# Earlier loads, two fences and moved buffers in an eight-core attention and feed-forward layer

## The reference

```python
D = 1024; H = 16; HIDDEN = 3072
# attention; its input is a normalised x
xn = layernorm(xin) * ln_g + ln_b
q = xn @ Wq.T + bq; k = xn @ Wk.T + bk; v = xn @ Wv.T + bv
q = softmax(q per head, over the head's 64 columns)
k = softmax(k, over the tokens)
attn = einsum('bnhd,bnhl->bhdl', k, v)      # one 64x64 matrix per head
y = einsum('bnhd,bhdl->bnhl', q, attn)
attn_out = xin + y
# layer
x = x + attn_out(xin = norm(x))
h = silu(norm(x) @ wg.T) * (norm(x) @ wu.T) # wg, wu, wd are int32, times 1/127
x = x + h @ wd.T
```

## Time and profile before

| | us |
|---|---|
| median of 2 runs | 4600.26 (4599.89 to 4600.62) |
| profiled execution, its own time | 4595.73 |
| span of that execution, slowest core (core 4) | 4594.2 |
| spans of the other cores | 4571.0 to 4594.0 |
| TensorE busy on core 4 | 3643.5 (79% of the span) |
| VectorE, ScalarE busy | 1269.6, 636.6 |

### The profile page before, as it was taken

How to read it: one execution, slowest core, us unless ns; L and a number is a source line. 1 busy time by engine, 2 the same in 40 slices (tenths; PEclk the granted TensorE clock), 3 DMA queues, 4 the chain that set the end, 5 groups by cost and what they waited for, 6 DMA issues and landing times.

```text
span 4594.2 us, 60873 instructions; the slowest of 8 cores (4571.0 to 4594.2 us)
## 1 busy us (share of the span) xinstructions
PE 3643.5 (79%) x22512; PEld 2464.3 (54%) x22800; DVE 1269.6 (28%) x3078; ACT 636.6 (14%) x1092; POOL 168.9 (4%) x295
## 2 busy tenths in 40 slices
PE   0369788866537888785254699999999999999998
PEld 0234334345533343345253477777777777777776
DVE  0232321234543213214254122222222222222222
ACT  0221221211112212211011000000000000000000
POOL 0000000000000000000000000000000000000000
PEclk9989899985558998896555799999999999999999
DMA  9721111143432112124843300000000000000000
GB/s 117 135 65 60 69 69 53 60 128 109 124 106 69 65 55 72 58 84 125 170 123 107 74 29 29 29 29 29 6 24 29 28 29 29 29 29 29 29 10 10
DMA packets 229040, 289.25 MB, mean 63 GB/s; under 512 B 83653, under 2 KB 182085, under 8 KB 226122
## 3 DMA queue, kind: packets, MB, share of 16 engines
q1 hardware_dynamic: 136218, 134.32, 10.6%
q0 software_dynamic: 33904, 136.33, 10.4%
q10 hardware_dynamic: 58624, 14.69, 2.0%
HBM read 167.86 MB, written 136.31 MB: 66 GB/s over the span
## 4 chain that ended last, share of the span: by engine, by line
PE 73%; DVE 11%; issue 4%; another core or an unknown queue 4%; ACT 3%; ACTq 2%; DMA 1%; DVEq 1%; SPq 1%; POOL 0%; POOLq 0%
PE pb L1051 29%; PE pb L604 14%; PE pb L1020 14%; PE pb L545 9%; DVE h_st L887 3%; PE pb L747 2%; ACTq L94 2%; PE pb L800 1%; DVE n_t L511 1%; DVE ek_r L739 1%; ACT h1n_t L907 1%; DVE xnT_lo L519 1%; DVE hnT_lo_st L818 1%; PE pb L731 1%
## 5 line engine op out<-in xcount | busy, mean ns | idle before, releaser
L1051 PE MATMUL pb<-hnT_hi_b,wgT 128*128 128x256 bf16 x3072 | 838.2, 273 | 48.2 <-DMA h_b<-s_h 48.2
L1051 PE MATMUL pb<-hnT_lo_b,wgT 128*128 128x256 bf16 x3072 | 838.2, 273 | 0.0
L1051 PE MATMUL pb<-hnT_hi_b,wuT 128*128 128x256 bf16 x3072 | 838.0, 273 | 0.0
L1051 PE MATMUL pb<-hnT_lo_b,wuT 128*128 128x256 bf16 x3072 | 838.0, 273 | 0.0
L1064 DVE SCALAR_TENSOR_TENSOR g_t<-pb,g_t 128x256 f32<-128x256 f32 x384 | 163.1, 425 | 1484.2 <-ACT g_t L1060 1423.5
L1060 ACT ACTIVATE g_t<-pb 128x256 f32<-128x256 f32 x384 | 147.2, 383 | 1859.4 <-PE pb L1051 1859.3
L1051 PEld LDWEIGHTS pb<-hnT_hi_b,wgT 128*128 128x128 bf16 x3072 | 300.9, 98 | 122.8 <-issue 48.8
L1051 PEld LDWEIGHTS pb<-hnT_lo_b,wgT 128*128 128x128 bf16 x3072 | 300.8, 98 | 74.3 <-issue 0.3
L1051 PEld LDWEIGHTS pb<-hnT_hi_b,wuT 128*128 128x128 bf16 x3072 | 300.9, 98 | 35.1
L1051 PEld LDWEIGHTS pb<-hnT_lo_b,wuT 128*128 128x128 bf16 x3072 | 300.9, 98 | 35.1
L545 PE MATMUL pb<-wvT_hi,xnT_hi 128*128 128x512 bf16 x486 | 168.8, 428 | 189.1 <-DVE v_stg L572 179.1
(11 more groups left out here) (150 smaller groups left out, 4448.1 us busy)
## 6 DMA issues: line engine op xcount, KB each, us to landing
x_r<-x SPq DMA_DIRECT2D x32, 512.0 KB, 4.0
s_r<-r_r POOLq DMA_DIRECT2D x32, 512.0 KB, 4.8
s_v<-v_stg POOLq DMA_DIRECT2D x32, 512.0 KB, 2.9
s_qT<-qT_stg POOLq DMA_DIRECT2D x64, 256.0 KB, 3.3
s_kT<-kT_stg POOLq DMA_DIRECT2D x64, 256.0 KB, 2.7
kTe<-s_kT SPq DMA_DIRECT2D x16, 1024.0 KB, 4.9
v_p<-s_v SPq DMA_DIRECT2D x16, 1024.0 KB, 6.0
qT_c<-s_qT SPq DMA_DIRECT2D x32, 512.0 KB, 6.8
```

The costliest lines, as they stand in the source:

```text
L1051: hc=hc, bsl=bsl, st=st, sp=sp: e.matmul(pb[bnk][:, 0:256], wtt[:, d, hc * 128:(hc + 1) * 128], xt.ap()[:, bsl, d, :], start=st, stop=sp),
```

## The change

- Two loads of x (the first two chunks of the first sequence) are put at the head of SyncE's queue, ahead of the identity, and `S1` uses them instead of its own.
- `pw_f` gets four slots instead of two; `ptmp` keeps two.
- Buffers of phase 3 move up so that they no longer overlap those of phase 2; wdT becomes one buffer of 24 columns, and the feed-forward's other buffers change places with it.
- The eight early wdT loads on ScalarE's queue are dropped; all 24 go to SyncE's queue behind the last fence.
- `prefetch_ffn_blocks`, called behind `emit_early_ffn_loads`, puts the hi and lo loads of blocks 0 and 1 on SyncE's queue at the end of phase 2 of the second sequence; the feed-forward uses them.
- The fence after phase 2 of the first sequence is dropped.

```diff
@@ buffers @@
-    qT_c = A("qT_c", [128, 2, 8, 128], F32, offset=P1 + 28 * KB)
-    r_c = A("r_c", [128, 2, D], F32, offset=P1 + 36 * KB)
-    h1_st = A("h1_st", [128, 2, D], F32, offset=P1 + 44 * KB)
-    h1n_t = A("h1n_t", [128, 2, D], F32, offset=P1)
+    qT_c = A("qT_c", [128, 2, 8, 128], F32, offset=P1 + 40 * KB)
+    r_c = A("r_c", [128, 2, D], F32, offset=P1 + 48 * KB)
+    h1_st = A("h1_st", [128, 2, D], F32, offset=P1 + 56 * KB)
+    h1n_t = A("h1n_t", [128, 2, D], F32, offset=P1 + 64 * KB)
...
-    pw_f = A("pw_f", [128, 2, D], F32, offset=P1 + 28 * KB)
+    pw_f = A("pw_f", [128, 4, D], F32, offset=P1 + 28 * KB)
...
-    wdT_a = A("wdT_a", [128, 8, D], BF16, offset=176 * KB)
-    wdT_b = A("wdT_b", [128, 16, D], BF16, offset=112 * KB)
-    hnT_hi_b = A("hnT_hi_b", [128, 2, 8, 256], BF16, offset=144 * KB)
-    hnT_lo_b = A("hnT_lo_b", [128, 2, 8, 256], BF16, offset=152 * KB)
+    hnT_hi_b = A("hnT_hi_b", [128, 2, 8, 256], BF16, offset=112 * KB)
+    hnT_lo_b = A("hnT_lo_b", [128, 2, 8, 256], BF16, offset=120 * KB)
+    wdT_t = A("wdT_t", [128, 24, D], BF16, offset=128 * KB)
...
@@ prologue @@
+    pre_x0 = {}
+    for c0 in range(2):
+        pre_x0[c0] = P.dma("sync", x0_r[:, c0, :], x_in[c0 * 128:(c0 + 1) * 128, :])
     m_ident = P.dma("sync", ident[:], ident_in[:, :])
...
-    pw_free = [[m_gcol], [m_bcolf]]
+    pw_free = [[m_gcol], [m_bcolf], [], []]
...
-            sl = (wi * 8 + rb) % 2
+            sl = (wi * 8 + rb) % 4
...
+            psl2 = sl % 2
...
@@ phase 1, S1 @@
-            mx = P.dma("sync", x0, x_in[tok0:tok0 + 128, :],
-                       waits=x0_res[sl].free)
+            if s == 0 and c < 2:
+                mx = pre_x0[c]
+            else:
+                mx = P.dma("sync", x0, x_in[tok0:tok0 + 128, :],
+                           waits=x0_res[sl].free)
...
@@ emit_early_ffn_loads @@
-        for hc in range(8):
-            mw[("d", hc)] = P.dma(
-                "scalar", wdT_a[:, hc, :], s_wd[0:D, hc * 128:(hc + 1) * 128],
-                waits=[m_cast["d"]] + deps, transpose=True)
...
+    def prefetch_ffn_blocks():
+        (ek_res2, kTe_res2, ekq_res2, vp_res2, _, _) = ph2_state[1]
+        ph2done = (vp_res2[0].free + vp_res2[1].free
+                   + kTe_res2[0].free + kTe_res2[1].free)
+        for b in range(2):
+            t0b = b * 256
+            mhi = P.dma("sync", hnT_hi_b[:, b % 2, :, :],
+                        s_hnT_hi[:, :, t0b:t0b + 256].transpose([1, 0, 2]),
+                        waits=m_hnT_store[b] + ph2done)
+            mlo = P.dma("sync", hnT_lo_b[:, b % 2, :, :],
+                        s_hnT_lo[:, :, t0b:t0b + 256].transpose([1, 0, 2]),
+                        waits=m_hnT_store[b] + ph2done)
+            ffn_pre[b] = [mhi, mlo]
@@ stages @@
             emit_early_ffn_loads()
+            prefetch_ffn_blocks()
             P.fence(pre)
+        elif nm.startswith("p2"):
+            pass
         else:
             P.fence()
...
@@ feed-forward @@
-    m_wd = {hc: mw[("d", hc)] for hc in range(8)}
-    for hc in range(8, 24):
+    m_wd = {}
+    for hc in range(24):
         m_wd[hc] = P.dma(
-            "sync", wdT_b[:, hc - 8, :], s_wd[0:D, hc * 128:(hc + 1) * 128],
+            "sync", wdT_t[:, hc, :], s_wd[0:D, hc * 128:(hc + 1) * 128],
             waits=[m_cast["d"]], transpose=True)
...
+        if b in ffn_pre:
+            mhi, mlo = ffn_pre[b]
+        else:
...
```

More of the change, by code:

```diff
@@ L246, in build @@
     wuT = A("wuT", [128, 8, HID], BF16, offset=64 * KB)
-    wdT_a = A("wdT_a", [128, 8, D], BF16, offset=176 * KB)
-    wdT_b = A("wdT_b", [128, 16, D], BF16, offset=112 * KB)
-    hnT_hi_b = A("hnT_hi_b", [128, 2, 8, 256], BF16, offset=144 * KB)
-    hnT_lo_b = A("hnT_lo_b", [128, 2, 8, 256], BF16, offset=152 * KB)
[L251 to L254, removed]
+    hnT_hi_b = A("hnT_hi_b", [128, 2, 8, 256], BF16, offset=112 * KB)
+    hnT_lo_b = A("hnT_lo_b", [128, 2, 8, 256], BF16, offset=120 * KB)
+    wdT_t = A("wdT_t", [128, 24, D], BF16, offset=128 * KB)
+    g1_t = A("g1_t", [128, 2, 256], F32, offset=176 * KB)
+    hmT_hi = A("hmT_hi", [128, 4, 256], BF16, offset=178 * KB)
+    hmT_lo = A("hmT_lo", [128, 4, 256], BF16, offset=180 * KB)
+    out_stg = A("out_stg", [128, 2, D], F32, offset=182 * KB)
     h1_b = A("h1_b", [128, 4, D], F32, offset=0)
     def wdT(hc):
-        return wdT_a.ap()[:, hc, :] if hc < 8 else wdT_b.ap()[:, hc - 8, :]
+        return wdT_t.ap()[:, hc, :]
     pb = [nc.alloc_psum_tensor(f"pb{i}", [128, 512], F32) for i in range(8)]
@@ L322, in build @@
             pw_free[sl] = trs[:]
[L323 to L327, removed]
-                waits=[trs[1]] + ptmp_free[sl])
+            psl2 = sl % 2
+            mtc0 = P.op("scalar", lambda e, psl2=psl2: e.activation(
+                out=ptmp[:, psl2, 0:512], in_=pb[6][:], func=AF.Copy),
+                waits=[trs[0]] + ptmp_free[psl2])
+            mtc1 = P.op("vector", lambda e, psl2=psl2: e.tensor_copy(
+                out=ptmp[:, psl2, 512:1024], in_=pb[7][:]),
+                waits=[trs[1]] + ptmp_free[psl2])
             bank[6].free = [mtc0]
             bank[7].free = [mtc1]
-            mhiw = P.op("scalar", lambda e, sl=sl, w=w, rb=rb: e.activation(
+            mhiw = P.op("scalar", lambda e, psl2=psl2, w=w, rb=rb: e.activation(
                 out=wT[(w, "hi")].ap()[:, :, rb * 128:(rb + 1) * 128],
-                in_=ptmp.ap()[:, sl, :].rearrange("p (a b) -> p a b", b=128),
+                in_=ptmp.ap()[:, psl2, :].rearrange("p (a b) -> p a b", b=128),
                 func=AF.Copy), waits=[mtc0, mtc1])
-            mlow = P.op("vector", lambda e, sl=sl, w=w, rb=rb: e.tensor_sub(
+            mlow = P.op("vector", lambda e, psl2=psl2, w=w, rb=rb: e.tensor_sub(
                 out=wT[(w, "lo")].ap()[:, :, rb * 128:(rb + 1) * 128],
-                in0=ptmp.ap()[:, sl, :].rearrange("p (a b) -> p a b", b=128),
+                in0=ptmp.ap()[:, psl2, :].rearrange("p (a b) -> p a b", b=128),
                 in1=wT[(w, "hi")].ap()[:, :, rb * 128:(rb + 1) * 128]),
                 waits=[mhiw])
-            ptmp_free[sl] = [mlow]
+            ptmp_free[psl2] = [mlow]
             m_wT[(w, rb)] = [mhiw, mlow]
@@ L980, in build @@
         t0 = b * 256
-        mhi = P.dma("sync", hnT_hi_b[:, bsl, :, :],
-                    s_hnT_hi[:, :, t0:t0 + 256].transpose([1, 0, 2]),
-                    waits=m_hnT_store[b] + hb_res[bsl].free)
-        mlo = P.dma("sync", hnT_lo_b[:, bsl, :, :],
-                    s_hnT_lo[:, :, t0:t0 + 256].transpose([1, 0, 2]),
-                    waits=m_hnT_store[b] + hb_res[bsl].free)
+        if b in ffn_pre:
+            mhi, mlo = ffn_pre[b]
+        else:
+            mhi = P.dma("sync", hnT_hi_b[:, bsl, :, :],
+                        s_hnT_hi[:, :, t0:t0 + 256].transpose([1, 0, 2]),
+                        waits=m_hnT_store[b] + hb_res[bsl].free)
+            mlo = P.dma("sync", hnT_lo_b[:, bsl, :, :],
+                        s_hnT_lo[:, :, t0:t0 + 256].transpose([1, 0, 2]),
+                        waits=m_hnT_store[b] + hb_res[bsl].free)
         mh1l = []
```

11 lines of the change are left out of this document (6 added, 5 removed).

## The result

The changed kernel is faster by about one per cent: the ratio of after to before is 0.9901, with a 95% interval of 0.988 to 0.9921, which on the scale of before is 4600.26 x 0.9901 = 4554.7 us. The forecast was 4565 with 4546 to 4588, a change of under 2%. The profiled execution took 4553.37 us, its span is 4551.8 us (core 0; the others 4529.8 to 4545.9).

The account below looks back on a forecast made before the run. TensorE holds 73% of the chain that ended last, so only its standstills could be won. +12 - 6.6 - 3 - 37 = -35 (rounded) from 4595.73 gave 4561, or 4565 on the median's scale; range 4546 to 4588.

Parts of the forecast that it names:

- the likeliest case: Whole kernel: the forecast itself, 4565 us with 4555 to 4575 as its own range, chance 0.66.
- The -35: Whole kernel: rounded sum of prologue +12, first entry -6.6, second entry -3 and start of the feed-forward -37 us.
- four packets of x get through before the first cast packet occupies the engine: Prologue: estimate that only four x packets pass ahead of the casts, leaving the first weight block late; +12 us.
- 42 turns: Prologue: SyncE's line up to the first weight block, against 36 turns during the casts; first block at about 184 us.
- rival 1: Prologue: x, identity and rows pass before the casts, or four waiting loads get more share; costs nothing, 4553 us, chance 0.16.
- -6.6: First entry into phase 3: without the fence, early fetches let TensorE go straight on, saving its 6.62 us idle time.
- -3 forecast: Second entry into phase 3: dropped wdT_a loads -10.8, block loads +8, sum -3 us, bounds -10.8 and +8.4.
- +8 for the block loads: Second entry: four block loads (2.1 MB) take DMA time from ScalarE's transposing loads, near their 7.4 us of transfer.
- rival 2: Second entry: block loads stretch four ScalarE issues, +8 instead of -3; 4576 us, 4583 without first-entry gain; chance 0.12.
- -37 forecast: Start of the feed-forward: loads already in place, only the fence left, TensorE begins at about 2525 us; bounds -36 and -38.
- Rival 3: Feed-forward block 0: TensorE waits for down weights, all 24 loaded after phase 3; 4614 us at 7.27 each; chance 0.03.
- a slow drain: Prologue: draining the rest of SyncE's line takes ten microseconds more, bound +22; the range's upper end 4588 adds 5.

Follow-up runs that it names:

- the two controls: Chip D: the kernel before, unchanged, and the changed kernel without early x loads but with four pw_f slots; first bias product at 258.49 and 257.97 us.

## Why the prediction was right or wrong

The side, the size and the places were right; the point was 10 us too slow (4565 against 4554.7), and 4554.7 is just outside the likeliest case's own range of 4555 to 4575. The -35 was made of four terms, two of which were mis-sized.

**The prologue: the step that failed.** The prediction's sentence was that "four packets of x get through before the first cast packet occupies the engine". All eighteen did. The DMA rows of the fourth microsecond (3 to 4 us), first of the kernel before, then of the changed one, and then the changed one's first 8 us:

```profile
q0 software_dynamic: 13, 0.43, 468.6%
q1 hardware_dynamic: 1, 0.00, 0.1%
```

```profile
q1 hardware_dynamic: 89, 0.36, 93.0%
```

```profile
q0 software_dynamic: 16, 0.52, 59.3%
q1 hardware_dynamic: 288, 1.05, 54.9%
```

In the kernel before, 13 cast packets start between 3 and 4 us, and one of SyncE's. With x flowing, no cast packet starts until 5 us. The first 16 cast packets start from 5.43 to 7.81 us, and none of them ends before 10.75. The 288 packets of SyncE's queue are x and nothing else (2 x 128 rows and 2 x 16 completions, 18 to an engine); the last of them starts at 7.80, and the identity's first at 10.73. So no packet of x stood behind a cast packet, and it is the same on the other seven cores (x's last packets start at 6.1 to 8.0 us, at most 0.02 us before the last engine's first cast packet).

The line at the moment that counts was therefore not 42 turns but 46 - 18 = 28. From 6 us to the first block it is (132.33 - 6)/4.95 = 25.5 turns, and two of the 28 packets went at next to no cost, since each of the first two casts ends with a packet of 4 bytes on every engine (at 62 to 65 and 121 to 124 us). By this count the late issue of the weights (63.15 us) cost nothing: other rows were still in line on that engine. Two blocks were through before the casts ended instead of none, and the loss was 5.3 instead of 12 us. I had taken the casts' start from before, where nothing stood against it. Of rival 1 the half came about: x slipped through, the identity and the rows did not (the identity landed 49.5 us after its issue).

The Trainium skill, "DMA: Bandwidth & Descriptors", section "Latency and other measured facts", gives about 1 us to the first byte of a DMA that GpSimd issues. Before the change that fits (issued at 1.58 to 2.26 us, first packet at 3.03); in the changed kernel it was 3 to 6 us, so the measurement decides. Why the casts start later there is not shown. The Trainium skill, "DMA: Bandwidth & Descriptors", section "Queues, rings and completion order", has each engine go round the queues that it has work for. Here 18 packets of one queue went to none of the other on each engine: either the casts' packets were not there yet, or the engine did not go round, and no run tells which.

All else in that part held: the turn of 4.95 us and nine turns a load (44.2 us from the first to the second block, 44.6 worked out), 3.34 us a block afterwards, no gain from four slots (0.5 us between the two controls), and none from having x early. Without early x the prologue keeps its old length.

**First entry: mechanism right, size too small.** The step was "-6.6", TensorE's idle time in the earlier trace rows. It was mis-sized twice. The row was that of core 4, and 6.62 is nearly the smallest of the eight cores (6.5 to 10.2, mean 7.93, and now -0.19: -8.1). And behind TensorE's pause I counted nothing, though the stretch from there to ScalarE's first own instruction was 14.56 us with the fence and is 12.83 without (14.56 again with the fence put back). That stretch is 11.5 us on three of the eight cores, 12.1 on a fourth, and 14.0 on the other four. The difference is TensorE's clock: in the first 5.5 us of phase 3 it was granted 1.00 on the three, 0.69 on the fourth and 0.50 on the four (1.00 is the level of 2.4 GHz, 0.50 that of 1.2), and the sixteen small products take 1.84 us on the former four cores and 3.41 on the others (3.54 or 3.55 on every core before, at 0.50 behind the pause). Cores 0 and 2, columns as in the earlier trace rows:

```profile
1091.35:1096.85 5.50, 5.50 (x27) 5.50 (x27) 0.99 (x4) 0.00 (x0) 0.00 (x0) 0.50 0.00 0
```

```profile
1086.44:1091.94 5.50, 5.50 (x52) 5.50 (x51) 2.77 (x11) 0.00 (x0) 0.00 (x0) 1.00 0.05 13
```

So on half of the cores the low clock behind the pause went with the pause. On the others the clock stood at 0.50 in the ten microseconds before as well; why is not shown.

**Second entry: right within its scatter.** -3 forecast, -3.6 measured. That the two agree to 0.6 us is luck: five executions with the block loads at this place take 85.0, 86.4, 86.6, 87.6 and 90.9 us, and two of the kernel before 88.6 and 92.4; their means differ by 3.2. The parts hold too: +8 for the block loads, of which moving them away shows 7.4 and 7.5. Against the 79.2 and 78.85 without the block loads, the mean 90.5 of the kernel before makes the eight wdT_a loads worth 11.4 (10.8 forecast). The single 11 us issue that rival 2 feared was there, but the sum over 32 loads did not follow it: ScalarE's queue lost about the time of the bytes. The Trainium skill, "DMA: Bandwidth & Descriptors", section "Issuing engines are not separate DMA queues", says that DMAs of different engines share the same 16 DMA engines; the trace agrees, with these 7.4 us.

**Start of the feed-forward: right.** -37 forecast, -36.9 measured; start at 0.45 us behind the last store's landing, and no wait for a down weight. Rival 3 was far off: 24 loads were issued in 38.57 us, 1.61 each, against the 5.22 in which TensorE uses one up. What the prediction did not say is that the order alone would have brought 27 of the 37.

**Sum.** +5.3 - 9.9 - 3.6 - 36.9 = -45.1 against -35: 6.7 us of the difference are the prologue's packet count, 3.3 the first entry. The time lies nearest to rival 1's 4553, but by another sum: the 5.3 us that the prologue cost after all and the 3.3 more at the first entry partly cancel, which is luck. The stated range was narrower than its own bounds, since its upper end adds 5 us for a slow drain where the prologue's bound has 10. And a change of under 2% can be told from none here: the interval of the ratio ends at 0.9921.

## What to carry to other kernels

Where large memory-to-memory transfers share the DMA engines with small loads, count packets ahead of the load that matters, take the start of the large transfers from a run in which the same queue is busy, and ask first whether the large transfers must run there at all: moved and cut into pieces, these were worth 163 us, thirty times what the order of the small ones was. A wait's price is a mean over all cores, and part of it is the clock that TensorE is granted behind the pause. Before loading ahead, look at what the load stands behind in its queue; and a queue of loads that blocks an engine with work of its own is better spread out on an engine without any (57 us here, for the engine and the spreading together).

## What the runs showed of the hardware that was not expected

- The casts' first packets start 2 to 4 us later when SyncE's queue is already moving x, just behind x's last: 0 of 89 packets from 3 to 4 us were theirs, against 13 of 14 without x; once both run, they alternate one for one. x issued at 1.06 us lands in 5.7 us, issued at 3.04 us in 94.0.
- Issuing 32 transposing loads holds the second entry for 57 us when ScalarE issues them (78.85, with no block loads beside them, against 21.35), and costs nothing that shows in phase 3 when SyncE does, three to a chunk.
- A fence costs about 10 us, the late loads behind it included: 9.6 at the second entry without transposing loads, 9.9 at the first, of which 8.1 stand in TensorE's row.
